# Softplus as Exp, Ln and a clip in a Mamba tower: the bias moved into a product, and the next norm moved by one position

## The reference

```python
for _ in range(4):
    x = mamba_block(simple_rmsnorm(x), ...)
# in mamba_block:
dbl = u @ W_x
dt = dbl[..., :dt_rank]
delta = jax.nn.softplus(dt @ W_dt + b_dt)
A = -jnp.exp(A_log)
def step(h, inp):
    u_t, d_t, B_t, C_t = inp
    h = jnp.exp(d_t[..., None] * A) * h + (d_t * u_t)[..., None] * B_t[:, None, :]
    y = jnp.einsum('bds,bs->bd', h, C_t)
    return (h, y)
```

## Time and profile before

| | |
|---|---|
| median of 3 runs | 2142.24 us (2139.98 to 2143.46) |
| the profiled execution's own time | 2141.26 us, of which its span is 2139.5 us |
| busy in the span | PE 94%, PEld (weight loads) 67%, DVE 70%, ACT 68%, POOL 69% |
| ACT_TABLE_LOAD | 65: 31 at L546, 16 at L508, 16 at L519, 2 others |
| mean granted TensorE clock | 0.983 |

### The profile page before, as it was taken

The page is one execution under the profiler, slowest core; times in us unless marked ns, Lnnn a source line. Parts: engine busy times, 40 slices in busy tenths (PEclk is TensorE's granted clock), DMA queues, the critical chain, the costliest instruction groups (busy, mean ns, idle before and its releaser), DMA issues.

```text
span 2139.5 us, 30859 instructions
## 1 busy us (share of the span) xinstructions
PE 2021.1 (94%) x11952; PEld 1440.0 (67%) x11952; DVE 1500.3 (70%) x1509; ACT 1448.3 (68%) x2294; POOL 1483.4 (69%) x845
## 2 busy tenths in 40 slices
PE   6989899999999999999999999999998889999997
PEld 3457677777777777877777777777777754444443
DVE  1368988889898989898988889898988860120101
ACT  0268898888989888988898988988898721000000
POOL 0039898989898998989898989898989940000000
PEclk9989999999999999999999999999999999999999
DMA  5211112111111111111112111211112410000000
GB/s 186 90 60 41 50 42 70 42 61 46 65 40 61 46 62 63 42 68 41 61 42 70 42 61 41 69 41 61 40 51 82 145 59 11 0 30 0 10 0 20
DMA packets 34137, 113.13 MB, mean 53 GB/s; under 512 B 6148, under 2 KB 8836, under 8 KB 33480
## 3 DMA queue, kind: packets, MB, share of 16 engines
q1 hardware_dynamic: 33992, 111.17, 15.3%
HBM read 95.95 MB, written 15.20 MB: 52 GB/s over the span
## 4 chain that ended last, share of the span: by engine, by line
PE 45%; POOL 18%; DVE 13%; issue 11%; ACT 11%; DMA 1%; SPq 0%; DVEq 0%; POOLq 0%; ACTq 0%
POOL hid L419 13%; PE b_ps L1110 8%; DVE hid L858 8%; PE y_all L1121 6%; ACT dub_t L559 5%; ACT hid L546 5%; PE y_all L1219 5%; PE b_ps L1219 5%; POOL dub_t L410 4%; DVE u L733 3%; PE y_all L922 3%; PE bank_b L1003 2%; PE y_all L1128 2%; PE y_all L1232 2%; PE bank_b L1018 2%
## 5 line engine op out<-in xcount | busy, mean ns | idle before, releaser
L858 DVE TENSOR_TENSOR_SCAN hid<-hid,b_ps 128x512 f32<-128x512 f32 x1024 | 1213.8, 1211 | 200.0 <-PE b_ps L1110 178.7
L419 POOL TENSOR_TENSOR hid<-hid,c_rep 128x1024 f32<-128x1024 f32 x512 | 1209.8, 2395 | 159.6 <-DVE hid L858 159.3
L1110 PEld LDWEIGHTS b_ps<-ident,dub_t 128*128 128x128 f32 x4096 | 485.6, 143 | 367.8 <-issue 218.3
L1110 PE MATMUL b_ps<-ident,dub_t 128*128 128x128 f32 x4096 | 631.5, 277 | 61.2 <-DVE hid L858 56.1
L546 ACT ACTIVATE hid<-delta,neg_a 128x512 f32<-128x512 f32 x1024 | 652.9, 711 | 0.4
L1121 PE MATMUL y_all<-ident,hid 128*128 128x128 f32 x4096 | 617.9, 274 | 19.7 <-POOL hid L419 19.6
L559 ACT ACTIVATE dub_t<-du_t,b_t 128x512 f32<-128x512 f32 x768 | 490.3, 712 | 57.8 <-PE b_ps L1110 56.1
L1121 PEld LDWEIGHTS y_all<-ident,hid 128*128 128x128 f32 x4096 | 481.2, 142 | 26.1 <-POOL hid L419 26.1
L410 POOL TENSOR_SCALAR dub_t<-du_t,b_t 128x512 f32<-128x512 f32 x256 | 173.8, 714 | 0.0
L733 DVE SCALAR_TENSOR_TENSOR u<-bank_b,conv_w_sb,u 128x511 f32<-128x511 f32 (+2 forms) x192 | 139.7, 728 | 0.7
L1003 PE MATMUL bank_b<-xn,w_in_sb 128*128 128x512 f32 x256 | 134.0, 611 | 3.3 <-DVE u L733 3.3
(11 more groups left out here) (192 smaller groups left out, 1770.5 us busy)
## 6 DMA issues: line engine op xcount, KB each, us to landing
c_rep<-bc_dram SPq DMA_DIRECT2D x128, 512.0 KB, 3.7
hid<-x_t SPq DMA_DIRECT2D x4, 2048.0 KB, 8.9
x_dram<-x_out SPq DMA_DIRECT2D x16, 512.0 KB, 2.8
xt<-x_dram SPq DMA_DIRECT2D x15, 512.0 KB, 3.6
h_dram<-hid SPq DMA_DIRECT2D x4, 512.0 KB, 3.3
out<-y_d SPq DMA_DIRECT2D x4, 512.0 KB, 2.6
x_dram<-hid SPq DMA_DIRECT2D x3, 512.0 KB, 2.7
c_rep<-x_dram SPq DMA_DIRECT2D x3, 512.0 KB, 5.9
```

Of the source, the lines that this page charges most:

```text
L419: nc.gpsimd.tensor_tensor(part, part, c_rep[:, n % 2, s % GROUP, :].unsqueeze(1) .broadcast_to([P, HALF, SEQ]), ALU.mult).then_inc(hc_read ...
L858: nc.vector.tensor_tensor_scan(hid[:, i % RING, d, :], hid[:, i % RING, d, :], b_ps[d % 2][:, :], 0.0, ALU.mult, ALU.add)\
L1110: last = nc.tensor.transpose(b_ps[d % 2][:, c * P:(c + 1) * P], dub_t[:, i % DUB, c, d * P:(d + 1) * P], ident[:, :])
```

## The change

The diff, cut to what moves work:

```diff
--- before.py
+++ after.py
@@ SP: b_dt goes into row 96 of w_dt_sb, behind DVE's memsets
-                    sp.dma_start(vec_sb[:, 1, :], b_dt).then_inc(weights_in, 16)
+                    sp.wait_ge(pad_ready, 4)
+                    sp.dma_start(w_dt_sb[XPROJ:XPROJ + 1, :], b_dt.unsqueeze(0)).then_inc(weights_in, 16)
@@ POOL
-                                if live(k + 1) and (s, half) == (6, 0):
+                                if live(k + 1) and (s, half) == (6, 1):
                                     times_u(k + 1, 0)
-                                if live(k + 1) and (s, half) == (7, 0):
+                                if live(k + 1) and (s, half) == (7, 1):
                                     times_u(k + 1, 1)
@@ ACT
-                    def softplus(k, d):
+                    def delta_exp(k, d):
                         act.wait_ge(wdt_done, NI * k + d + 1)
-                        nc.scalar.activation(delta[:, k % 2, d, :], (bank_a if d % 2 == 0 else bank_b)[:, :], ACT.Softplus,
-                                             bias=vec_sb[:, 1, d:d + 1]).then_inc(delta_ready, 1)
+                        nc.scalar.activation(delta[:, k % 2, d, :], (bank_a if d % 2 == 0 else bank_b)[:, :], ACT.Exp)\
+                            .then_inc(exp_ready, 1)
+
+                    def delta_log(k, d):
+                        act.wait_ge(exp_ready, NI * k + d + 1)
+                        nc.scalar.activation(delta[:, k % 2, d, :], delta[:, k % 2, d, :], ACT.Ln, bias=1.0).then_inc(log_ready, 1)
...
                             if s == 8 and live(k + 1):
-                                softplus(k + 1, 0)
-                                softplus(k + 1, 1)
+                                delta_exp(k + 1, 0)
+                                delta_exp(k + 1, 1)
+                                delta_log(k + 1, 0)
+                                delta_log(k + 1, 1)
...
                             if s == 4 and live(k + 1):
                                 gate(k + 1, 2)
                                 gate(k + 1, 3)
+                                nc.scalar.preload_act_table_set("natural_log_exp_and_others")
...
                             if s == 8 and live(k + 1):
-                                softplus(k + 1, 2)
-                                softplus(k + 1, 3)
+                                delta_exp(k + 1, 2)
+                                delta_exp(k + 1, 3)
+                                delta_log(k + 1, 2)
+                                delta_log(k + 1, 3)
@@ DVE
+                    dve.wait_ge(pad_ready, 2)
+                    nc.vector.memset(dbl[XPROJ:XPROJ + 1, :], 1.0).then_inc(pad_ready, 2)
...
+                    def softplus(k, d):
+                        dve.wait_ge(log_ready, NI * k + d + 1)
+                        nc.vector.scalar_tensor_tensor(delta[:, k % 2, d, :], (bank_a if d % 2 == 0 else bank_b)[:, :], 60.0,
+                                                       delta[:, k % 2, d, :], ALU.max, ALU.min).then_inc(delta_ready, 1)
...
+                    SOFTPLUS_AT = {(7, 0): 0, (7, 1): 1, (8, 0): 2, (8, 1): 3}
...
+                                if live(k + 1) and at in SOFTPLUS_AT:
+                                    softplus(k + 1, SOFTPLUS_AT[at])
-                                if live(k + 2) and at == (8, 2):
+                                if live(k + 2) and at == (8, 3):
                                     normalize(k + 2)
@@ PE
-                                if live(k + 2) and at == (8, 1):
+                                if live(k + 2) and at == (8, 2):
                                     spread_norm(k + 2)
```

More of the change, by code:

```diff
@@ L179, in build @@
             wdt_done = sem("wdt_done")
+            exp_ready = sem("exp_ready")
+            log_ready = sem("log_ready")
             delta_ready = sem("delta_ready")
@@ L975, in _ @@
                     pe.wait_ge(weights_in, 8 * 16)
-                    pe.wait_ge(pad_ready, 2)
+                    pe.wait_ge(pad_ready, 4)
                     def squares(k):
@@ L1423 @@
         a = np.asarray(inputs[name])
-        laid[name] = a.reshape(-1, P).T if a.ndim == 1 else a
+        laid[name] = a.reshape(-1, P).T if a.ndim == 1 and name != "L0_attn_b_dt" else a
     arrays, args = {}, []
```

## The result

| | before | after |
|---|---|---|
| median, runs of the same job | 2142.85 us (2139.98 to 2145.69, 4 runs) | 2203.91 us (2203.25 to 2204.74, 4 runs) |
| profiled execution, its span | 2141.26, 2139.5 us | 2203.92, 2202.1 us |
| step without a clock drop | 100.22 us | 104.41 us |
| ACT_TABLE_LOAD | 65 | 34 |

What follows compares the result with a forecast made beforehand. Bound: the chain of last-ending waits across ACT, DVE, PE and POOL, not one engine's work. Full steps 48.75, `k` = 0 about 3.0, `k` = 14 0.4, start 0.5: sum 52.6 on 2141.26, said as 2194 us; range 2161 to 2208.

Steps and rivals of the forecast that it cites:

- the replay: Recomputed times of one step's stretch after 1088 us from the earlier trace: full step 3.75 us longer; chance 0.64.
- 1, `to_delta` 2: At (7,1): PE waits for clip 0, behind DVE's scan of (7,0), and starts 0.82 us late.
- 2, `back` 2: At (8,0): PE waits for clip 2, behind DVE's scan of (8,0); 2.86 us late, PE standing for 2.0.
- 3, `spread_norm`: At (8,2): PE waits for clip 3 and goes on at 1101.04, 0.8 us more.
- 4, `in_x`: At (9,0): `normalize` stands behind the scan of (8,3), so `in_x` starts 4.4 us late.
- 5, scan of (9,2): On DVE: the scan is 4.1 us late; from here taps fill DVE without gaps until 1110.95.
- 6, first `times_c` behind `times_u`: At (10,0): POOL is 1.3 to 1.4 us late; PE, less 1.38 of slack, is 2.8 late and stays later.
- 7, `b_states` (11,0): Needs the scan of (10,2), 3.95 us late; with slack 0.2 it is 3.75 late, as is the full step.
- A: Rival: PE recovers its lateness, only POOL's own 1.4 us per step is left, 2162 us; chance 0.12.
- B: Rival: waits at (10,0) and (11,0) absorb nothing, step 4.4 us longer, 2207 us; chance 0.12.
- C: Rival: ACT decides, its 0.8 us saved per step counts, 12 us gained, 2130 us; chance 0.07.
- D: Rival: table switches on ACT cost the drain too, 3.6 us gained per step, 2087 us; chance 0.01.

Runs made afterwards that it cites:

- clip23_early: Changed kernel with clip 2 moved behind the scan of (7,3) and clip 3 behind that of (8,0), nothing else; 2180.74 us.
- tiny_release: Changed kernel with each clip replaced, at its place in DVE's queue, by a four-column read raising the same semaphore; min with max(z, 60) left out; 2178.82 us.
- norm_back: Changed kernel with spread_norm back at (8,1) and normalize back behind the scan of (8,2); 2208.97 us.
- exp_only: Kernel before with Exp in place of Softplus, logarithm left out, no Ln or clip, two table loads less per step; 2140.56 us, ratio 0.9998.
- clips_early: Changed kernel with clips behind scans (6,3), (7,0), (7,2), (7,3), each Ln after its Exp, norm and second `times_u` put back; 2157.83 us.
- norm_late: Kernel before with only spread_norm moved to (8,2) and normalize behind the scan of (8,3); 2165.08 us.
- no_clip: Changed kernel without DVE's clips (min with max(z, 60) left out); Ln raises `delta_ready`, Exp frees the banks for PE; 2160.66 us.

## Why the prediction was right, and what was mis-sized

**The mechanism.** Every wait that the replay placed is in the trace, and within 0.4 us of its time. On the scale of the earlier trace rows (times of after less 144.23):

| item | forecast | after |
|---|---|---|
| 1, `to_delta` 2 | 1091.64 | 1091.59 |
| 2, `back` 2 | 1098.02 | 1097.96 |
| 3, `spread_norm` | 1101.04 | 1101.11 |
| 4, `in_x` | 1104.50 | 1104.66 |
| 5, scan of (9,2) | 1107.75 | 1108.07 |
| 6, first `times_c` behind `times_u` | 1105.98 | 1106.05 |
| 7, `b_states` (11,0) | 1116.17 | 1116.57 |

PE's waits were 0.60, 1.76 and 0.75 us where 0.8, 2.0 and 0.8 were forecast, POOL's lateness (item 6) about 1.4 as forecast, and PE's wait for POOL at (10,0) is gone, as said. That is tried and not only read off: two clips one position earlier took away half of `back`'s wait and 1.64 of the 4.19 us (clip23_early), and tiny instructions at the clips' places kept most of the waits (tiny_release).

**The size.** The step grew by 4.19, not 3.75. Items 1 to 3 are right to 0.1; the error enters in three small pieces behind them. The scan of (8,3), ahead of `normalize`, was taken to follow the scan before it; in fact it waited for its `b_states`, which stands behind the late `spread_norm` on PE:

```profile
1246.51 1.22 DVE L878 TENSOR_TENSOR_SCAN hid<-hid,b_ps 128x512 f32<-128x512 f32 x1 [0.19 <-PE b_ps L1132]
```

That makes `in_x` 0.16 later than forecast. From `in_x` to the scan of (9,2) the replay has 3.25 us (1104.50 to 1107.75). The trace has 3.41, and the kernel before had 3.55 (1100.08 to 1103.63), so the replay let the lateness shrink from 4.4 to 4.1 there and gave no row for it. PE's instructions of this stretch:

```profile
1249.86 0.60 PE L1132 MATMUL b_ps<-ident,dub_t 128*128 128x128 f32 x4
...
1250.73 1.02 PE L1025 MATMUL bank_b<-xn,w_in_sb 128*128 128x512 f32 x2
1251.59 0.60 PE L1132 MATMUL b_ps<-ident,dub_t 128*128 128x128 f32 x4
```

The pair of `in_x` matmuls that comes after a wait is 0.97 ahead of its follower (1248.89 to 1249.86), the one that doesn't is 0.86 ahead (1250.73 to 1251.59): 0.1 of the 0.16 that come in here. The last 0.08 is at (11,0), where `b_states` began 0.15 behind the end of the scan and not 0.06. Together 0.4 on top of the 3.75, over 13 steps 5.7 us.

**The sum by its terms.** The profiled spans differ by 62.6 us, where the sum has 52.6:

| term | forecast | measured |
|---|---|---|
| start and `k` = 0 | 3.5 | 2.5 |
| 13 full steps | 48.75 | 54.5 |
| clock drops in them | none | 2.3 (4 times 1.67, less 3 times 1.44) |
| `k` = 14 | 0.4 | 0.3 |
| behind the last step | none | 3.0 |

The part behind the last step isn't touched by the change. Its windows, of before and of after:

```profile
1616.00:2139.50 523.50, 490.93 (x1854) 268.46 (x1852) 168.25 (x188) 122.95 (x197) 130.95 (x81) 0.96 0.10 36
```

```profile
1675.80:2202.10 526.30, 492.07 (x1852) 268.15 (x1850) 169.67 (x188) 122.95 (x197) 130.85 (x81) 0.95 0.10 35
```

The work is the same, the granted clock 0.95 instead of 0.96: at half clock PE spent 44.9 us in the one and 50.8 in the other. That needs no cause in the change: tiny_release and norm_back, whose programs are those of the changed kernel here, take 523.3 and 523.1 us for the same stretch, as the kernel before does, and over all fourteen profiles it varies from 520.3 to 526.3. So these 3.0 us are no miss of the replay's mechanism; whether the change makes the longer form likelier, one profile for each kernel doesn't tell.

**The costs by themselves.** A clip took 665 ns (forecast from the tap's 729), and a follower came 0.58 us behind its start (forecast 0.64). Ln took 622 and a follower came 0.52 behind its start (taken as 0.61, from a bracket of 0.55 to 0.64 whose lower end was itself too high: the follower of the Silu comes 0.52 behind it). A load took 1283 as before. ACT's busy time in a full step without a drop fell by 0.6 us (88.0 to 87.4), where 0.8 was forecast. ACT went from waiting 59.1 us for `du_turn` to 89.7, so its saving became wait, as said.

**The rivals.** A (POOL alone, 2162) fell: PE isn't waiting for POOL anywhere in the stretch. B said that nothing is recovered between `in_x` and (11,0), 4.4 per step and 2207 us. Of the 4.58 us by which `in_x` was late 0.43 were recovered, where the replay had 0.67 (4.42 less 3.75), so the mechanism is nearer the replay. B's numbers, 4.4 for a step and 2207 for the time, were nearer than mine all the same, the time partly by the slower clock behind the last step. C and D fell in exp_only. The rule of the Trainium skill behind D (ScalarE: Activation LUTs, "What ACT_TABLE_LOAD costs": a drain of about 1380 ns on top of the load) isn't confirmed: by the page, two switches less should leave ACT 5.3 us per step more to wait in exp_only, as an estimate, and its idle time grew by 2.6 (12.2 to 14.8). In the trace of before ACT's idle time is 0.02 us in front of a load and 0.01 behind it.

## What to carry to other kernels

An instruction that frees a buffer belongs on an engine that is early at that place. Moving the release from ACT (done with block 2 at 1092.97, 2.2 us before PE wanted the bank) to DVE (whose queue stands behind a scan that itself waits for PE) made a loop between PE and DVE; of 4.2 us per step half was the order alone, 1.6 the added work. So before adding a cheap instruction to an engine with gaps, replay who waits for it, and try its place a few positions earlier: with the other moves of clips_early that took back 3.3 of the 4.2 us here, and 1.6 by itself for two clips and one position. And saving work on an engine that ends the stretch waiting gives nothing: look for its wait, and expect it to grow by about what was saved (2.6 us per step in exp_only).

## What the runs showed of the hardware

Two things I had not expected. First, a DVE elementwise instruction whose operands all lie in SBUF was held by POOL's instruction until that ended, whenever it began under one: 45 of 64 times in both kernels, with means over all 64 of 1601 ns (two inputs) and 1361 ns (one input, stride of two), where it takes 658 and 396 undisturbed. The same work with one input in PSUM took 665 with POOL just as busy. The same clip is thus cheap from the bank and dear from SBUF. Second, clock drops of 3.4 us can fall into every step of one length of step (102.4 us, in norm_late and no_clip) and into a few of another (1 to 8 of the 13 full steps at 99.75 to 104.6 us). Runs of the very same kernel then lay 26 and 29 us apart, with mean granted clocks from 0.985 to 0.973. A half microsecond per step, which the replay could tell, was covered by that in the time, and only the length of a step in the profile showed it.
